# The start of a two-layer block kernel: one block from the first load through the recurrent stage

## The reference, cut to what matters

```
mod = silu(c) @ wmod                      # 4 x (6*256): sa, ca, ga, sb, cb, gb
ga, gb = sign(ga)*max(|ga|, 0.25), ...
x = x + ga * attn(layernorm(x) * (1 + ca) + sa)
x = x + gb * ffn(layernorm(x) * (1 + cb) + sb)
```

## Time and profile before

| | us |
|---|---|
| median of 3 runs | 1109.02 (1106.84 to 1109.79) |
| the profiled execution, whole | 1106.67 |
| its span | 1104.9 |
| TensorE busy | 1045.2 (95%) |
| VectorE busy | 696.2 (63%) |
| ScalarE busy | 553.2 (50%) |
| GpSimd busy | 434.7 (39%) |
| first gate product of step 0, after the span's start | 81.10 |
| first gate product of step 1 | 118.52 |

### The profile page before, as it was taken

How to read it: one execution, slowest core, us unless ns; L and a number is a source line. 1 busy time by engine, 2 the same in 40 slices (tenths; PEclk the granted TensorE clock), 3 DMA queues, 4 the chain that set the end, 5 groups by cost and what they waited for, 6 DMA issues and landing times.

```text
span 1104.9 us, 26014 instructions
## 1 busy us (share of the span) xinstructions
PE 1045.2 (95%) x10262; PEld 756.2 (68%) x10262; DVE 696.2 (63%) x2084; ACT 553.2 (50%) x1428; POOL 434.7 (39%) x391
## 2 busy tenths in 40 slices
PE   5988999999999999999999899999999999999978
PEld 2747788878887855574648667675867576757646
DVE  5219889889889952213232776756675676667774
ACT  2438777887787742212132453535454445444531
POOL 1022203303514711101003574756567565778720
PEclk8589999999999999999999899999999999999999
DMA  9300000000000002800003000300030002100202
GB/s 338 129 1 1 2 1 0 0 0 0 0 1 2 2 1 49 281 1 1 1 0 77 20 20 21 77 20 20 21 77 21 20 21 57 41 20 21 77 3 78
DMA packets 24207, 42.19 MB, mean 38 GB/s; under 512 B 6576, under 2 KB 14768, under 8 KB 22704
## 3 DMA queue, kind: packets, MB, share of 16 engines
q1 hardware_dynamic: 24112, 40.87, 12.4%
HBM read 21.98 MB, written 2.10 MB: 22 GB/s over the span
## 4 chain that ended last, share of the span: by engine, by line
PE 51%; DVE 5%; ACT 2%; issue 1%; POOL 0%; DVEq 0%
PE quad L1948 9%; PE quad L1597 7%; PE quad L1990 7%; PE quad L2010 7%; PE quad L1993 5%; PE quad L1892 5%; PE quad L2024 5%; PE quad L2088 1%; PE quad L1956 1%; ACT act_probs L2246 1%; DVE act_probs L2346 1%; PE quad L1483 1%; ACT act_probs L2255 1%; PE quad L1911 1%; DVE wq_wo L2360 1%
## 5 line engine op out<-in xcount | busy, mean ns | idle before, releaser
L2599 POOL TENSOR_TENSOR act_probs<-act_probs,rden 128x512 f32<-128x512 f32 (+3 forms) x128 | 171.0, 1339 | 155.9 <-DVE rden L2365 155.8
L2246 ACT ACTIVATE act_probs<-act_probs,neg_max 128x256 f32<-128x256 f32 (+3 forms) x256 | 140.8, 552 | 82.6 <-DVE neg_max L2346 82.3
L1948 PEld LDWEIGHTS quad<-hT,ug_queries 128*128 128x128 f32 x1024 | 120.5, 194 | 30.6 <-issue 18.6
L1948 PE MATMUL quad<-hT,ug_queries 128*128 128x128 f32 x1024 | 132.2, 283 | 3.0 <-ACT act_probs L2255 2.2
L2346 DVE CUSTOM_DVE_ANT_0 act_probs<-quad,mask 128x256 f32<-128x256 f32 (+3 forms) x256 | 114.9, 486 | 6.4 <-PE quad L1993 6.0
L1597 PE MATMUL quad<-hT,ug_raw_switch 128*128 128x512 f32 x256 | 115.6, 602 | 0.0
L1990 PE MATMUL quad<-ckvT,ug_raw_switch 64*128 64x512 f32 (+3 forms) x512 | 105.6, 480 | 6.9 <-DVE neg_max L2346 6.9
L2365 DVE RECIPROCAL rden<-den 128x2 f32<-128x2 f32 x128 | 20.6, 161 | 121.1 <-ACT act_probs L2246 120.9
L1612 DVE SCALAR_TENSOR_TENSOR act_probs<-quad,ws_up,silu_keys 128x512 f32<-128x512 f32 x32 | 24.0, 751 | 102.4 <-ACT silu_keys L1607 102.4
L1597 PEld LDWEIGHTS quad<-hT,ug_raw_switch 128*128 128x128 f32 x256 | 48.1, 193 | 55.5 <-issue 54.7
L1607 ACT ACTIVATE silu_keys<-quad,ws_gate 128x512 f32<-128x512 f32 x32 | 22.0, 687 | 120.5 <-PE quad L1597 120.5
(11 more groups left out here) (318 smaller groups left out, 2361.8 us busy)
## 6 DMA issues: line engine op xcount, KB each, us to landing
rope_swapped<-gate SPq DMA_DIRECT2D x120, 64.0 KB, 2.0
wmod<-in_wmod SPq DMA_DIRECT2D x2, 1536.0 KB, 9.9
x_pairs<-in_x SPq DMA_DIRECT2D x2, 1024.0 KB, 9.8
x_rows<-x_pairs SPq DMA_DIRECT2D x8, 256.0 KB, 4.8
wq_wo<-in_wq_nopeT SPq DMA_DIRECT2D x1, 2048.0 KB, 8.6
wq_wo<-in_wo SPq DMA_DIRECT2D x1, 2048.0 KB, 12.9
down_raw_out<-x_pairs SPq DMA_DIRECT2D x16, 128.0 KB, 2.3
ug_queries<-in_switch_w SPq DMA_DIRECT2D x1, 2048.0 KB, 7.8
```

The costliest lines, as they stand in the source:

```text
L1948: mm = nc.tensor.matmul(out[:, P * i:P * i + P], w[:, kt, HP * half + i, :], k.hT[:, kt, b, cols], start=(kt == 0), stop=(kt == KT - 1))
L2246: nc.scalar.activation(tile, tile, ACT.Exp, bias=neg_max[:, r, e:e + 1], scale=-1.0, accum_out=den[:, r, e:e + 1])\
L2599: nc.gpsimd.tensor_tensor(tile, tile, rden[:, t % RING, :].unsqueeze(2).to_broadcast([P, 2, cols]), ALU.mult)\
```

## The change

The start block goes; its work stands in the recurrent block's programs.

- **Loads.** Both modulation matrices are cut in thirds of 0.5 MB and loaded into tiles that the ffn's weights use later (ug_raw_switch, down_raw_out). Order now: conditions, first third of layer 0, x in four quarters (two before and two behind the unit matrix, w_qkv and the rates' weights), the other five thirds, the states, small tables; then, when the modulations are multiplied, the ffn's weights. The gates are spread over partitions by 16 DMAs from rows.
- **Modulation.** `Modulations` takes blocks of the matrix (128 x 128) as stationary operand and silu(c) (4 columns) as moving one, so that mod comes out in columns: 24 places per layer of two kinds (shift, scale: kept as they are; gates: guarded, turned into rows once). Only the first shift and scale come first (8 products), the other 40 products stand behind the transposes of step 0's q, k, v, in front of its gate products.
- **Norm.** `StartNorm` goes by two chunks per group. Groups 0 and 1 (chunks 0 to 3) stand before the first projection; groups 2 and 3 are turned and modulated inside step 0, all through bank 6, one after the other (START in INNER and TAKEN).
- **Rates.** Four tiles ahead of step 0, the other 12 inside it: six products with w_lr as stationary operand (32 columns) and 512 tokens as moving one, a copy, four transposes, exponential and logarithm; their last nine operations on VectorE stand between step 0 and the loop, with the scaling of w_proj and of the sign tables.
- **Step 0.** Projections of chunks 0 and 1 read hT itself. Half of chunk 1's stand behind the gate products. The root of the first q and k norms is a power on GpSimd; VectorE scales q and k of chunk 0. The norms of the start state are summed and rooted in step 0.

The core of the diff:

```diff
-        for n in range(3):
-            for kt in range(KT):
-                mm = self.k.nc.tensor.matmul(self.k.bank[4 + n][0:B, :], self.silu[:, kt, :], self.w[:, kt, 2 * D * n:2 * D * n + 2 * D],
-                                             start=(kt == 0), stop=(kt == KT - 1))
+    def make(self, pe, l, parts):
+        for part in parts:
+            n, half = divmod(part, 2)
+            for m in range(KT):
+                at, lo = self.column(l, part, m), D * half + P * m
+                for kt in range(KT):
+                    mm = self.k.nc.tensor.matmul(self.bank[:, at:at + B], self.w[l][n][:, kt, lo:lo + P], self.silu[l][:, kt, :],
+                                                 start=(kt == 0), stop=(kt == KT - 1))
+        return mm
...
+    def modulate(self, act, g, kt, src):
+        act.wait_ge(self.turned, 2 * g + kt + 1)
+        for b in range(B):
+            to, view, scale, shift = self.views(g, kt, b, src)
+            op = self.k.nc.scalar.activation(to, view, ACT.Identity, scale=scale, bias=shift)
+        op.then_inc(self.taken, 1)
...
+    def project_rest(self, pe):
+        for kt in range(KT):
+            for g in range(3):
+                mm = self.k.nc.tensor.matmul(self.k.bank[6][self.PAD * g:self.PAD * g + self.PAD, :], self.w[:, kt, :],
+                                             self.tokens[:, kt, 4 * P * (g + 1):4 * P * (g + 2)], start=(kt == 0), stop=(kt == KT - 1))
+        mm.then_inc(self.zT_made, 1)
...
-    INNER = ((A, 0), (A, 1), (OUT_ROWS, 1), (A, 2), (A, 3), (AA, 0), (A, 4), (AA, 1), (A, 5), (TURN_V, 0), (AA, 2), (OUT_ROWS, 0), (AA, 3), (Y, 0), (AA, 4), (AA, 5), (TURN_QK, 0), (Y, 1),
+    INNER = ((A, 0), (A, 1), (OUT_ROWS, 1), (START, 0), (A, 2), (A, 3), (AA, 0), (A, 4), (AA, 1), (START, 1), (A, 5), (TURN_V, 0), (AA, 2), (OUT_ROWS, 0), (START, 2), (AA, 3), (Y, 0), (AA, 4), (AA, 5), (START, 3), (TURN_QK, 0), (Y, 1),
...
+                    elif ph == START and first:
+                        if n == 1:
+                            pe.wait_ge(mods.rows_taken, 1)
+                        elif 2 <= n < 6:
+                            pe.wait_ge(first_norm.taken, 2 + n)
+                        if n == 0:
+                            mods.make_rows(pe)
+                        elif n < 5:
+                            first_norm.turn(pe, 2 + (n - 1) // 2, (n - 1) % 2, bank[6])
+                        elif n == 5:
+                            rates.project_rest(pe)
+                        else:
+                            rates.turn_rest(pe)
...
+            pe.wait_ge(k.consts_set, N_CONSTS)
+            mods.make_first(pe)
+            pe.wait_ge(k.eye_in, 16)
+            for g in range(2):
+                for kt in range(KT):
+                    first_norm.turn(pe, g, kt, bank[NORM_PLACES[g][kt]])
+            pe.wait_ge(qkv_in, 16)
+            first_norm.wait_chunks(pe, 0)
+            project_qk(0, 0)
+            project_qk(0, 1)
+            rates.project_first(pe)
             project_v(0)
-            for i in range(PAIRS):
-                project_qk(i)
+            pe.wait_ge(s["qkv_acted"], 1)
+            project_qk(1, 0)
             pe.wait_ge(s["qkv_acted"], 3)
-            project_v(1)
-            for i in range(PAIRS):
-                project_qk(i)
             turn_v(0, 0)
-            turn_qk(0, 0, 4)
-            turn_qk(0, 1, 6)
+            pe.wait_ge(first_norm.taken, 2)
+            turn_qk(0, 0, 1)
+            turn_qk(0, 1, 3)
+            pe.wait_ge(rates.step, 1)
+            mods.make_rest(pe)
+            mods.make_next(pe)
             step(0, first=True)
...
             step(0, first=True)
+            rates.finish(dve, 1)
+            dve.wait_ge(proj_in, 32)
+            nc.vector.tensor_scalar(w_proj[:], w_proj[:], onorm[:], None, ALU.mult)
+            ffn.scale_signs(dve)
             with dve.Fori(1, NCH - 1) as t:
                 step(t)
```

More of the change, by code:

```diff
@@ L120, in allocate_residents @@
     k.eye_in, k.consts_set = k.sem("eye_in"), k.sem("consts_set")
-    k.x_in = [k.sem(f"x_in{h}") for h in range(2)]
+    k.x_in = [k.sem(f"x_in{g}") for g in range(4)]
     k.norms_of, k.ffn = Norms(k), FeedForward(k)
[L125 to L141, removed]
-    def load_c(self, sp):
-        sp.dma_start(self.cT[:], self.k.ins[f"cT{self.l}"]).then_inc(self.c_in, 16)
-    def load_w(self, sp):
-        sp.dma_start(self.w[:], self.k.ins[f"wmod{self.l}"]).then_inc(self.w_in, 16)
@@ L185, in guard_gates, with column @@
-    def guard_gates(self, dve):
-        v, step, gate, sign = self.k.nc.vector, self.step, self.gate[:], self.sign[:]
-        raw = self.rows[:].rearrange("b (a m d) -> b a m d", a=2, d=D)[:, :, GATE_A, :]
-        dve.wait_ge(self.rows_taken, 3 * self.l + 3)
+        for l in range(2):
+            self.k.nc.scalar.activation(self.silu[l][:], self.cT[l][:], ACT.Silu).then_inc(self.silu_done, 1)
+    def column(self, l, part, m):
+        if part in self.GATES:
+            return B * (4 * self.GATES.index(part) + 2 * m + l)
+        return B * (8 + 8 * l + KT * self.KEPT.index(part) + m)
@@ new lines, in make_rows, with take_rows @@
+    def make_rows(self, pe):
+        pe.wait_ge(self.step, 5)
+        pe.wait_ge(self.taken, 6)
+        for n in range(2 * KT):
+            mm = self.k.nc.tensor.transpose(self.bank[0:2 * B, P * n:P * n + P], self.gate[:, 2 * B * n:2 * B * n + 2 * B], self.k.eye[:])
+        mm.then_inc(self.rows_made, 1)
+    def take_rows(self, act):
+        act.wait_ge(self.rows_made, 1)
+        self.k.nc.scalar.activation(self.rows[0:2 * B, :], self.bank[0:2 * B, :], ACT.Copy).then_inc(self.rows_taken, 1)
@@ L987, in take @@
                     nc.scalar.activation(out[:, q, :], src, ACT.Copy, scale=scale).then_inc(taken[q], 1)
[L989 removed]
+                if more and not first:
                     silu_qk(t + 1, 0)
[L991 removed]
+                elif not more:
                     ffn.take_fold(act, 0, bank[FOLD_BANK[0]])
@@ L995, in step @@
                         take_weight(t - 1, q)
-                if more:
+                if more and not first:
                     silu_qk(t + 1, 1)
-                else:
+                elif not more:
                     ffn.take_fold(act, 1, bank[FOLD_BANK[1]])
@@ L1048, in step @@
                     ffn.take_fold(act, 4, bank[FOLD_BANK[4]])
+                if first:
+                    rates.logarithm(act, 1)
+                    load_table(ACT.Sqrt)
                 def square_state(q):
@@ L1240, in step @@
                         norm_out(t - 1)
+                    if first and n == 3:
+                        rates.start(dve, 1)
+                if first:
+                    rates.one_more(dve, 1)
                 def update(q):
```

663 lines of the change are left out of this document (343 added, 320 removed).

## The result

The changed kernel takes 1102.18 us (median of 5 runs, 1101.59 to 1103.49), the kernel before 1109.02 (5 runs as well): a ratio of 0.9946, with a 95% interval from 0.9932 to 0.996. It is faster by 6.8 us on the medians, 4.4 to 7.5 by the interval, and the forecast was 1090. The profiled execution lasted 1103.49, its span is 1101.7.

A forecast was written before the change was run, and what follows sets the result against it. The prediction took TensorE, busy 95% of the span, as the bound and asked what its start cost. Terms -33.9 + 3.2 + 1.5 + 9.0 + 1.5 = -18.7 gave a span of 1086.2, on the median 1090, range 1079 to 1098.

The forecast's parts named there:

- the gates' DMAs: Sixteen small copies said to run beside step 0, their reader waiting only before step 2; no cost was put on them.
- The loads and the first 8 products: Start of the kernel: first load of 0.5 MB landed at 6.5, first 8 products from 6.5 to 9.9.
- The first gate product, 47.2: Step 0's first gate product at 47.2 instead of 81.1, a term of -33.9 us, most narrow records at low clock.
- the rival with a high clock: Clock stays at 2.4 GHz through the 80 narrow records: first gate product at 40.1, time 1081; chance 20 in 100.
- Up to the first scaled matrix: Step 0, from the gates: +3.2 us for added VectorE work, +1.5 for the low clock at the beginning.
- From there to the first state update, +9.0: Step 0: modulations +5.0, rates +2.0, VectorE's wait behind a table load +1.7, and 0.3 for last transposes.
- Behind the updates: hidden, by 0.2: Step 0: ScalarE's added logarithm and table loads end at 29.1, against 29.3 for VectorE's reductions, so cost nothing.
- the drain that the prediction weighed: ScalarE table switches: by the Trainium skill a 1.38 us drain, some 2.6 us more in step 0; the trace showed none.
- Step 1, +1.5: VectorE's 3.7 us of rates and scaling before step 1, less idle time of 1.5 and 0.7, leaves +1.5 us.
- whatever moves the first gate product of step 1 moves the end by as much: Loop body and what follows are untouched, so any gain at step 1's first gate product, 118.52 before, reaches the end.
- From step 2 on the same 39: Later steps of the loop: each still takes 39 us, as before the change.
- step 0 could grow more: Rival: dearer modulations, strips that don't overlap, the logarithm's cover gone; +6 us, time 1096; chance 18 in 100.

The follow-up runs named there:

- x2: The changed kernel with twelve of the 16 gate copies issued only once step 3 has begun: 1086.80 us, and 1085.39 when run again.
- x4: The changed kernel with 16 DMAs of the same sizes, but each partition copying a row of its own (wrong gate values): 1085.91 us.
- x1: The changed kernel without the 16 gate copies and without GpSimd's wait for them (wrong gate values): 1086.34 us, ratio to before 0.9787.
- x5: The kernel before with 16 copies of exactly the changed kernel's sizes added, and GpSimd's wait for them: 1124.56 us, ratio 1.014.
- x7: The changed kernel with 12 of the 16 gate copies, gate 2 left out (wrong factors): 1093.56 us, ratio 0.986.
- x6: The changed kernel with each gate copy cut into one of 63 or 127 rows and one of a single row: 1094.33 us, ratio 0.9863.
- x8: x2 with layer 1's 24 modulation products moved from ahead of step 0's first gate product to behind its projections: 1082.42 us, and 1083.10 when run again.

## Why the prediction was wrong

The forecast was 1090, with a range from 1079 to 1098; the time is 1102.18. The step that failed is the one on the gates' DMAs, put at nothing because their only reader waits late; the runs show that they cost 15.4 to 15.8 us by holding up the instruction loads of TensorE. By the prediction's own steps:

- *The loads and the first 8 products.* Forecast 6.5; the first product stands at 6.27. Right.
- *The first gate product, 47.2.* It stands at 44.38. The narrow records took 15.03 us, forecast 15.7, at 0.50 for most of them: the choice of the low clock was right, and the rival with a high clock wrong. What is in front of them was 2 us shorter. So -36.7 in place of -33.9.
- *Up to the first scaled matrix.* 11.55 + 3.2 + 1.5 = 16.25 forecast; 44.38 to 60.65 is 16.27. Right.
- *From there to the first state update, +9.0.* 60.65 to 84.19 is 23.54, so +10.0. The four modulations took 1.50 to 1.51 each, as forecast:

```profile
65.03 1.50 ACT L272 ACTIVATE hT<-quad,modT,scale1T 128x128 f32<-128x128 f32 x4
...
72.77 1.51 ACT L272 ACTIVATE hT<-quad,modT,scale1T 128x128 f32<-128x128 f32 x4 [0.20 <-PE quad L260]
```

- *Behind the updates: hidden, by 0.2.* It was not hidden. Step 0 took 54.0 us, forecast 51.1. Of the 2.9 us that are missing 1.0 is the term above, and 1.9 came behind the updates (from the first update to the gates 14.23 us, before 12.32). With logarithm and table loads in front, ScalarE's column sums began 4.9 us after the first update, 2.4 before; VectorE waited 0.51 us for their root, and its first rescaling stood 8.04 us after the first update, 7.44 before. The other 1.3 us lie on TensorE, which waited 3.11 us for the scaled state (1.77 before) and whose window from 90 to 98 us is at 0.79 (the same in x2 and x4, 0.57 in x1; before, 110 to 118 us at 1.00). Each table load took 1.28 us and the function behind it started 1.29 to 1.30 after the load's start, so the drain that the prediction weighed does not show here either:

```profile
86.08 1.28 ACT L351 ACT_TABLE_LOAD   x1
87.38 0.26 ACT L351 ACTIVATE out_hidden<-out_hidden 128x72 f32<-128x72 f32 x1
87.66 1.28 ACT L927 ACT_TABLE_LOAD   x1
...
91.77 0.17 DVE L1265 SCALAR_TENSOR_TENSOR w_ne<-w_n,wnorm 128x12 f32<-128x12 f32 x1 [0.51 <-ACT w_n L1026]
...
92.98 1.97 PE L607 MATMUL quad<-eye,state 128*128 128x128 f32 x8 [3.11 <-DVE state L1271]
```

- *Together, at step 1.* The forecast's terms up to here put its first gate product at 98.3, and it stands at 98.42. That is luck as much as skill: 2.8 us too little gain in front and 2.9 too little growth in step 0 cancel.
- *Step 1, +1.5.* Without the copies (x1) it takes 39.24 us from gates to gates, as before (39.25). VectorE's last nine operations on the rates (96.32 to 98.95) lie ahead of the gates' data. Wrong by 1.5, in the good direction.
- *"The gates' DMAs (16 small ones) run beside step 0, their reader waits only before step 2."* This is the step that failed. They are not small (1.84 MB from eight rows of one tile, one partition at a time), they don't end in step 0 but just before 140, in step 1, and what they cost was not at their reader. I had asked who waits for them and not what else goes through the DMA engines. The diff had the numbers: 12 x 128 + 4 x 64 packets of 1 KB, each from a single partition. With it fell the sentence that whatever moves the first gate product of step 1 moves the end by as much: it came 20.1 us earlier and the last one 1.9.
- *"From step 2 on the same 39."* Right (39.2).

Some readings were off without weight: the page of before has a fourth slice at 8, the 23rd; the loads' rate between 9.09 and 11.42 is 0.43 MB/us and not 0.45; the distance called 0.86 is 0.84.

The price of that step is 15.8 us by x1, 15.4 by x2, and 15.6 by x5 from the other side. Without it, the profiled execution of x1 has a span of 1086.0, where the sum gave 1086.2. This too agrees in part by luck, since the 1.5 us of step 1 did not come and x1's stretch behind the last gate product was 1.5 us longer than before. On the medians, x1, x2 and x4 lie near 1086 where the sum gave 1090.3. So the other terms together were 4 us too pessimistic, the copies cost 15.8, and the miss of 12 is the difference. No rival named it. The nearest said that step 0 could grow more, and put the mechanism elsewhere.

The trace of before could not have given the size, since no DMA there reads one partition for many. The Trainium skill could: SBUF — State Buffer, under "Door 1: The DMA port swizzle", says that a DMA's bandwidth depends on how many of 16 ports its partitions reach, with 436 GB/s for all. One of 16 ports is, as an estimate from that page, 27 GB/s, and 68 us for 1.84 MB, with an end near 141. The trace agrees: 28 GB/s, and an end just before 140. Then the question which other traffic is on these engines until 140 would have been due.

## What to carry to other kernels

A DMA that spread one row over 64 or 128 partitions ran at the speed of reading one partition here and kept all 16 engines busy meanwhile: count its bytes at some 28 GB/s, and ask what else has to pass those engines. A program's instructions are among that: place bulk or slow DMAs where an engine repeats a loop, not where it meets new code, and look for rows released by "issue" that coincide with blocks of the instruction queue. Idle time of TensorE had a second price behind it here, in the clock: half as much again as the stops in the changed kernel, and more than the stop itself in x7.

## What the runs showed of the hardware

- Instruction blocks of 16 KB go through the DMA engines and wait there behind copies of data: stops of 2.5 to 6.1 us in step 1 of the changed kernel, 3.2 to 5.2 in x5, one of 3.6 in x7, none in step 1 of x1 to x4, nor in x6. TensorE starts again 2.2 to 2.5 us after the start of the block. In which order an engine serves its queues, and through which engine a block comes, was not measured.
- 1.8 MB from single partitions took 66 to 75 us, at 24 to 28 GB/s, whether the copies occupied 75% of the 16 engines (128 rows) or 10% (127 rows); in x2, in another order of rows, they ran at 37 GB/s; from 128 partitions the same bytes were through in some 12 us.
- A row less made a copy harmless to the instruction loads and some 13% slower in itself (x6: 75 us for all, in place of 66), so that GpSimd had to wait for it: -7.9 us against the change, where moving the copies gave -15.4.
- One program's time varied by 8.6 us (x8, 1078.76 to 1087.34), more than most edits here are worth. Its mean granted clock went with it (0.994 to 0.984), in the narrow products and also behind the last gate product; so its median says less than x2's.
